# Local attention in a 12-layer stack: products P V with 64 rows of keys and the queries' values as columns, P paired by DMA, O transposed on TensorE

## The reference

```python
q, k, v = split(x @ Wqkv, 3)                  # 128 channels -> 3 * 1024
q, k = l2norm(q) * qs, l2norm(k) * ksc        # over the 64 dimensions of a head
q, k = rotary(q), rotary(k)                   # cos, sin and scale tables by token
# blocks of 32 queries; each sees its own block and the one before, 64 keys
sim = (q_block @ concat(k_prev, k_block).T) * 8.0, masked
attn = softmax(sim)                           # 32 queries x 64 keys
out = attn @ concat(v_prev, v_block)          # 64 values per head
x = x + concat_heads(out) @ Wo                # in the kernel's state
x = x + (a * gelu(gate)) @ W2 + b2            # layer norm, W1 to 2 * 341, gated
```

## Time and profile before

| what | value |
|---|---|
| time, median of 3 runs | 4463.43 us (4456.26 to 4473.81) |
| time of the profiled execution | 4466.84 us |
| its span, first to last instruction | 4465.1 us |
| busy: PE, DVE, POOL, ACT | 4085.3, 3289.0, 2496.9, 2340.3 us |
| mean granted TensorE clock | 0.972 of full speed |
| tiles in the two stacks | 192 |

### The profile page before, as it was taken

How to read it: one execution, slowest core, us unless ns; L and a number is a source line. 1 busy time by engine, 2 the same in 40 slices (tenths; PEclk the granted TensorE clock), 3 DMA queues, 4 the chain that set the end, 5 groups by cost and what they waited for, 6 DMA issues and landing times. The chain is left out here.

```text
span 4465.1 us, 195370 instructions
## 1 busy us (share of the span) xinstructions
PE 4085.3 (91%) x89528; PEld 2450.9 (55%) x89528; DVE 3289.0 (74%) x4385; ACT 2340.3 (52%) x3044; POOL 2496.9 (56%) x2036
## 2 busy tenths in 40 slices
PE   6887899999999999999678877999999999999997
PEld 2322666666666666666333335666666666666664
DVE  7997678777777877788454436777787777777774
ACT  6885455555555555555234443455555555555553
POOL 0002677776777767776200006677676776767673
PEclk8999899999999999999789998999999999999998
DMA  0001111111112112111000011112112111111110
GB/s 19 1 1 45 44 53 35 53 46 46 52 31 60 42 42 59 33 32 32 12 1 1 1 36 41 53 33 60 42 39 55 40 50 47 43 52 38 32 36 21
DMA packets 92028, 162.87 MB, mean 36 GB/s; under 512 B 33997, under 2 KB 55241, under 8 KB 91209
## 3 DMA queue, kind: packets, MB, share of 16 engines
q1 hardware_dynamic: 91208, 150.36, 12.4%
HBM read 48.61 MB, written 1.05 MB: 11 GB/s over the span
## 5 line engine op out<-in xcount | busy, mean ns | idle before, releaser
L1102 PEld LDWEIGHTS banks<-f_P_T,f_V_previous 32*64 32x64 f32 x24576 | 482.9, 131 | 509.6 <-issue 486.9
L1102 PE MATMUL banks<-f_P_T,f_V 32*64 32x32 f32 x24576 | 578.5, 223 | 35.7 <-issue 34.8
L1102 PE MATMUL banks<-f_P_T,f_V_previous 32*64 32x32 f32 x24576 | 570.0, 227 | 28.1 <-issue 24.6
L1072 PE MATMUL banks<-f_wqkv,H 128*128 128x512 f32 x1152 | 568.4, 617 | 17.0 <-DVE f_rope_bk L1395 9.5
L1341 POOL TENSOR_TENSOR f_q_rotated<-f_rope_aq,f_rope_bq 128x1024 f32<-128x1024 f32 x192 | 454.6, 2368 | 231.4 <-DVE f_rope_bq L1395 231.0
L1072 PE MATMUL banks<-f_wqkv,G 128*128 128x512 f32 x1152 | 554.0, 603 | 0.6
L1392 DVE TENSOR_TENSOR f_rope_aq<-banks,f_rope 128x1024 f32<-128x1024 f32 x192 | 235.2, 1225 | 429.6 <-ACT f_sqq L1254 415.0
L1341 POOL TENSOR_TENSOR f_k_rotated<-f_rope_ak,f_rope_bk 128x1024 f32<-128x1024 f32 x192 | 451.9, 2354 | 165.9 <-DVE f_rope_bk L1395 165.8
L1328 POOL MEMSET f_kT<- 128x256 f32 x2 | 0.6, 312 | 838.7 <-POOLq L514 460.8
L1102 PEld LDWEIGHTS banks<-f_P_T,f_V 32*64 32x64 f32 x24576 | 440.6, 133 | 41.7 <-issue 40.5
L1126 PE MATMUL banks<-f_O_T,f_wo 128*128 128x128 f32 x3072 | 437.6, 289 | 4.9 <-issue 4.9
(11 more groups left out here) (204 smaller groups left out, 8489.5 us busy)
## 6 DMA issues: line engine op xcount, KB each, us to landing
f_V_previous<-f_V SPq DMA_DIRECT2D x192, 384.0 KB, 3.6
f_V_previous<-f_V SPq DMA_DIRECT2D x192, 128.0 KB, 2.3
f_wqkv<-in_L_ffn_Wqkv SPq DMA_DIRECT2D x48, 384.0 KB, 4.1
f_rope<-in_rope SPq DMA_DIRECT2D x24, 512.0 KB, 5.2
f_wo<-in_L_ffn_Wo SPq DMA_DIRECT2D x12, 512.0 KB, 5.2
f_w<-in_L_ffn_W SPq DMA_DIRECT2D x12, 341.0 KB
f_w<-in_L_ffn_W SPq DMA_DIRECT2D x24, 64.0 KB
xin<-in_L_attn_a_x SPq DMA_DIRECT2D x2, 512.0 KB, 5.0
```

The source lines that it names most:

```text
L1072: mm = nc.tensor.matmul(ps[:, o * BLK:(o + 1) * BLK], xs, w[:, c * INNER + o * BLK:c * INNER + (o + 1) * BLK], start=True, stop=True)
L1102: mm = nc.tensor.matmul(banks[i * DH:(i + 1) * DH, g * BLK + k * W:g * BLK + (k + 1) * W], of[n % 3][r, h * DH:(h + 1) * DH], PT[n % 2][r, ...
```

## The change

`values` takes 64 keys as rows. For a pair of neighbouring query blocks (64 tokens), `F` holds the transposed P of each block with the 64 keys that it sees below one another. The stationary operand is a 64 x 32 slice of `F`, the moving one 64 rows of V or Vp with a head's 64 values as columns. There are 64 products per tile and none accumulates. The result is O with tokens on partitions, in `PQ`. ACT copies it to `O`, PE transposes it in eight 128 x 128 transposes into `PK`, and ACT evacuates that to `OT`.

`F` is made from `PT`, of which there is one in place of two, by eight transfers per tile of 32 partitions and 2 KB each (SP), and therefore values, output projection and all feed-forward steps run one slot later. `E` is laid out by side (previous block, own block) instead of by head. The products stand in two halves: one after the v projection, one after the first two feed-forward pieces; the output projection is in one piece. V has four buffers.

```diff
-            def values(n, k0, k1):
-                for k in range(k0, k1):
-                    for now, of in ((0, Vp), (1, V)):
-                        for i in range(2):
-                            h = 2 * k + i
-                            for g in range(NG):
-                                r = slice(g * W, (g + 1) * W)
+            def values(n, j0, j1):
+                for j in range(j0, j1):
+                    for a in range(2):
+                        r = slice(a * 2 * W, (a + 1) * 2 * W)
+                        for t, of in ((0, Vp), (1, V)):
+                            for hh in range(2):
+                                h = hh * (HEADS // 2) + j
+                                c = (h % 2) * HP + h // 2
+                                g = 2 * hh + t
                                 mm = nc.tensor.matmul(
-                                    banks[i * DH:(i + 1) * DH, g * BLK + k * W:g * BLK + (k + 1) * W],
-                                    of[n % 3][r, h * DH:(h + 1) * DH], PT[n % 2][r, (i * HP + k) * 2 + now, :],
-                                    start=now == 0, stop=now == 1)
+                                    PQ[g * W:(g + 1) * W, a * BLK + j * DH:a * BLK + (j + 1) * DH],
+                                    F[n % 2][r, t, c * W:(c + 1) * W], of[n % len(of)][r, h * DH:(h + 1) * DH],
+                                    start=True, stop=True)
...
 # SP, at the head of a slot
+                if live(s - 2):
+                    sp.wait_ge(ppt.sem, ppt.at(n - 2))
+                    sp.wait_ge(o_mm.sem, o_mm.past(n - 4))
+                    for a in range(0, P, 2 * W):
+                        for t in range(2):
+                            for b in range(2):
+                                sp.dma_start(F[n % 2][a + b * W:a + (b + 1) * W, t, :],
+                                             PT[a + t * W:a + (t + 1) * W, b, :]).then_inc(pair_in[n % 2].sem, 16)
...
 # PE, the slot's second part
-                if live(s - 2):
-                    values(n - 2, 2, 4)
                 feed_second(s)
-                if live(s - 2):
-                    values(n - 2, 4, 6)
+                if live(s - 3):
+                    values(n - 3, HEADS // 4, HEADS // 2)
                 feed_third(s)
-                if live(s - 3) and s % TB != 1:
-                    out_part(s, 0, HP // 2)
-                if live(s - 2):
-                    values(n - 2, 6, 8)
+                if live(s - 4):
+                    out(s)
                 feed_fourth(s)
                 if live(s - 3):
-                    out_part(s, HP // 2 if s % TB != 1 else 0, HP)
+                    if live(s):
+                        pe.wait_ge(sqd.sem, sqd.at(n))
+                        pe.wait_ge(rot.sem, rot.at(n))
+                    else:
+                        pe.wait_ge(o_ev.sem, o_ev.past(n - 4))
+                    pe.wait_ge(o_cp.sem, o_cp.at(n - 3))
+                    for k in range(HP):
+                        mm = nc.tensor.transpose(PK[:, k * P:(k + 1) * P], O[:, k * P:(k + 1) * P], ident[:])
+                    mm.then_inc(o_tr.sem, 1)
...
 # ACT, at the head of a slot, ahead of the squares of q
+                if live(s - 4):
+                    act.wait_ge(o_tr.sem, o_tr.at(n - 4))
+                    act.wait_ge(y_mm.sem, y_mm.past(n - 6))
+                    nc.scalar.activation(OT[n % 2][:].rearrange("p a k t -> p (a k t)"), PK, ACT.Copy)\
+                        .then_inc(o_ev.sem, 1)
...
 # ACT, between V and the square of the centred block, E's exponential, Ln and Exp
+                if live(s - 3):
+                    act.wait_ge(o_mm.sem, o_mm.at(n - 3))
+                    act.wait_ge(o_tr.sem, o_tr.past(n - 4))
+                    nc.scalar.activation(O[:], PQ, ACT.Copy).then_inc(o_cp.sem, 1)
...
 # ACT, after Ln and Exp: the old evacuation of O_T is gone
-                if live(s - 2):
-                    act.wait_ge(o_mm.sem, o_mm.at(n - 2))
-                    act.wait_ge(y_mm.sem, y_mm.past(n - 4))
-                    nc.scalar.activation(OT[n % 2][:].rearrange("p g k t -> p g (k t)"),
...
 # DVE
-                    dve.wait_ge(o_mm.sem, o_mm.past(n - 4))
-                    nc.vector.transpose(PT[n % 2][:].rearrange("p h t -> p (h t)"), E[n % 2][:]).then_inc(ppt.sem, 1)
+                    dve.wait_ge(pair_in[(n - 3) % 2].sem, pair_in[(n - 3) % 2].past((n - 3) // 2))
+                    nc.vector.transpose(PT[:].rearrange("p b t -> p (b t)"), E[n % 2][:]).then_inc(ppt.sem, 1)
```

More of the change, by code:

```diff
@@ L901, in ffn_stack @@
         ri = sb("row_inverse", [P, HEADS])
-        PT = [sb(f"P_T{u}", [P, 2 * HEADS, W]) for u in range(2)]
-        OT = [sb(f"O_T{u}", [P, NG, HP, W]) for u in range(2)]
+        PT = sb("P_T", [P, 2, HEADS * W])
+        F = [sb(f"P_T_paired{u}", [P, 2, HEADS * W]) for u in range(2)]
+        O = sb("O", [P, INNER])
+        OT = [sb(f"O_T{u}", [P, 2, HP // 2, P]) for u in range(2)]
         xcs = sb("x_centered", [P, BLK])
@@ L1114, in hidden, with out @@
                                  start=True, stop=True).then_inc(sem, 1)
-            def out_part(s, k0, k1):
+            def out(s):
                 n = tile(s)
[L1119 to L1126, removed]
+                if (s - 4) % LAYER == 0:
+                    pe.wait_ge(wo_in.sem, wo_in.at(call * DEPTH + layer(s - 4)))
+                if not live(s - 1):
+                    pe.wait_ge(g_add.sem, g_add.past(n - 5))
+                pe.wait_ge(o_ev.sem, o_ev.at(n - 4))
+                for k in range(HP):
+                    hh, m2 = divmod(k, HP // 2)
+                    mm = nc.tensor.matmul(bank(4, P), wo[layer(s - 4) % 2][:, k, :],
+                                          OT[n % 2][:, :, m2, hh * 2 * W:(hh + 1) * 2 * W],
                                           start=k == 0, stop=k == HP - 1)
-                if k1 == HP:
-                    mm.then_inc(y_mm.sem, 1)
+                mm.then_inc(y_mm.sem, 1)
             def feed_first(s):
-                if (b := feed(s, 7)) is not None:
+                if (b := feed(s, 8)) is not None:
                     pe.wait_ge(g_add.sem, g_add.at(first + b * TB + TB - 1))
@@ L1136, in feed_first @@
                                      start=True, stop=True).then_inc(f_xc.sem, 1)
-                if (b := feed(s, 9)) is not None:
+                if (b := feed(s, 10)) is not None:
                     if b % NBLK == 0:
@@ L1275, in _ @@
                     squares(n, 1, k_mm, PK)
-                if (b := feed(s, 10)) is not None:
+                if (b := feed(s, 11)) is not None:
                     act.wait_ge(f_gev.sem, f_gev.at(blk(b)))
@@ L1457, in _ @@
                     nc.vector.tensor_scalar(var[:], bank(5), EPS, None, ALU.add).then_inc(f_eps.sem, 1)
[L1458 removed]
+                if (b := feed(s, 9)) is not None:
                     if b % NBLK == 0:
@@ L1474, in _ @@
                                                        src[rows, cols], ALU.add, ALU.add).then_inc(h_new.sem, 1)
-                if live(s - 3):
-                    dve.wait_ge(y_mm.sem, y_mm.at(n - 3))
-                    for rows, cols in halves(s - 3, P):
-                        nc.vector.tensor_tensor(state(s - 3)[rows, cols], bank(4, P)[rows], state(s - 3)[rows, cols],
+                if live(s - 4):
+                    dve.wait_ge(y_mm.sem, y_mm.at(n - 4))
+                    for rows, cols in halves(s - 4, P):
+                        nc.vector.tensor_tensor(state(s - 4)[rows, cols], bank(4, P)[rows], state(s - 4)[rows, cols],
                                                 ALU.add).then_inc(g_add.sem, 1)
-                if (b := feed(s, 13)) is not None and b >= SLOTS // TB - NBLK:
+                if (b := feed(s, 14)) is not None and b >= SLOTS // TB - NBLK:
                     dve.wait_ge(h_new.sem, h_new.at(blk(b)))
```

124 lines of the change are left out of this document (69 added, 55 removed).

## The result

The changed kernel takes 4600.79 us (median of 4 runs, 4596.13 to 4607.32) against 4460.92 us before: a ratio of 1.0308, 95% interval 1.0295 to 1.0321. It is slower by 3.1%, where 2.5% was forecast (4573 us).

What follows compares the result with a forecast made beforehand. PE bound before; after, the ring through ACT's copy of O: 18.28 us per slot against 17.79, 94 us, plus 10 for the ends, gives 4571, 4567 against the median, 4573 with a clock allowance; range 4475 to 4735.

Steps and rivals of the forecast that it cites:

- What bounds it before: In the kernel before, PE sets the pace: 17.50 us per slot in the best four, 17.79 on average.
- the margin of 0.72 us: In the kernel before, the gap from the end of POOL's multiplication of k to PE's transposes of k, in one slot.
- The step that decides, ACT's queue: ACT's copy of O, waiting for PE's late products, delays Ln and Exp: 5.26 us from V's end to Exp's, before 4.18.
- the upper of the two bounds: For half of the new products on PE: the old products' rate, 0.79 us, where 0.70 was taken.
- the ring: Loop of k's transposes, scores, V (PE), seeds (ACT), Newton, k's multiplication (POOL): 16.93 us before, mean 18.13 after.
- the transfers hide: SP's eight pairing transfers, 0.59 us per issue, land some 13 us before the products use them; no contention in sight.
- The rival of the clock: PE's clock falls after idling, 1.5 us on the ring: 4717 us in half of the slots, 4861 in all; chance 0.20.
- stalls of PE: Stalls inside PE's runs of matmuls, 0.29 us per slot before; 0.15 was kept, with bounds 0 and 0.29.
- The ends: At each stack's end the last tile passes added issues, landing, copy and transposes: 5 us per stack, 10 us in all.
- PE stays the bound: Rival: the copy of O is off the ring, so 17.0 to 17.1 us per slot, 4331 us; chance 0.08.
- The two cancel: Rival: the ring takes 17.8 us, so the time stays the same, 4463 plus or minus 22 us; chance 0.10.
- The products overlap less: Rival: PE's new products take twice the scores' rate, 1.41 us per half, 136 us more, 4709 us; chance 0.07.

Runs made afterwards that it cites:

- e5: Kernel before plus one unused ACT copy between V and E's exponential, released by V itself: 4460.41 us, ratio 0.9994.
- e6: Kernel before plus one unused ACT copy, released by three quarters of the products but placed behind Ln and Exp of the sums: 4464.27 us (one run).
- e1: Changed kernel with ACT's copy of O moved behind Ln and Exp of the sums: 4360.95 us, ratio 0.9779 to the kernel before.
- e2: Changed kernel with all 64 products ahead of the wait for V, ACT's order untouched: 4362.3 us, ratio 0.9781 to the kernel before.
- e4: Kernel before plus one unused ACT copy between V and E's exponential, released by three quarters of the products: 4770.78 us (one run).
- e3: Changed kernel without the eight pairing transfers and their waits, F a constant: 4580.4 us, ratio 1.0269 to the kernel before.
- e7: Kernel before plus eight transfers per tile like the pairing ones, into spare tiles nobody reads: 4490.63 us, ratio 1.007.

## Why the prediction was right, and where it was off

**What bounds it before, and the margin of 0.72 us.** That PE sets the pace is right: e5 and e6 leave the kernel before at 4460 and 4464 us with more work on ACT. The margin was read in one slot, and it is 0.73 us in two kinds of slot only (medians). Where POOL takes 5.44 us it is 0.48, and in the slot with two feed-forward products 0.20, and 0.15 of each goes to the handover when it is waited for. So even with ACT's queue clear, PE's own time could not be had in those two kinds of slot, and e1 gains next to nothing in them.

**The step that decides, ACT's queue.** Right, and shown from both sides: the copy's place (e1), its release (e2), and the copy without the change (e4 to e6). Its terms: V's end to the copy 2.90 forecast (2.09 and 0.81), 2.87 measured (medians over 80 slots); seeds' end 5.26 forecast, 5.22 measured, and 5.75 against 5.70 in the slot with the square. Two errors cancel in it, which is luck: half of the products takes 0.79 us, not 0.70 (the upper of the two bounds), and the feed-forward products, now undivided, 0.96 each, not 1.02.

**The size.** The mean slot was forecast at 18.28 us and is 18.59 in the window of 80 slots. Four terms of the ring were too small or left out:

- The scores take 1.55 us on average in place of 1.45 before (1.41 in the row that was used): 0.14. That the transfers hide was right for their landing; that they leave PE alone was not, and e3 prices it at 20 us at least. Their issue was off as well: 5.92 us for eight (median of 83 slots, 5.12 to 7.79), 0.74 each, not 0.59, though still covered. One of the long ones:

```profile
1414.69 7.25 SPq L1053 DMA_DIRECT2D f_P_T_paired<-f_P_T  x8
```

- POOL's end to PE's transposes is 0.15 us, not 0.05, and the k projection behind them starts after 0.90, not 0.87: 0.13. A handover that was never waited for cannot be read off a timeline.
- In one slot of four POOL's part takes 5.46 us, not 5.13: 0.08. It did so before as well (5.44 there); the row read was of another slot. What is longer is the instruction that runs beside DVE's scaling of the centred block, here POOL's multiplication of q, 2.23 us for 1.90:

```profile
1407.13 0.76 DVE L1504 SCALAR_TENSOR_TENSOR f_xn<-f_x_centered,f_ln_g_ln_b_b,f_var_then_rstd 128x512 f32<-128x512 f32 x1
```
```profile
1407.42 2.23 POOL L1389 TENSOR_TENSOR f_q_rotated<-f_q_rotated,f_inverse_norm 128x1024 f32<-128x1024 f32 x1
```

- The clock. In 7 of the 80 slots PE's clock fell to the lower of its two levels. Six are of the kind with two feed-forward products, and their period is 19.7 to 19.9 us in place of 18.3. PE had idled 1.13 and 0.86 us before, and then most of the k transposes and of the k projection ran at the lower level (the granted clock is 0.50 from 1223 to 1225 us in the slot shown, and 1.00 again from 1226):

```profile
1220.33 1.09 PE L1228 MATMUL banks<-ident,f_q_rotated 128*128 128x128 f32 x8 [1.13 <-POOL f_q_rotated L1389]
1222.28 1.72 PE L1234 MATMUL banks<-ident,f_k_rotated 128*128 128x128 f32 x8 [0.86 <-POOL f_k_rotated L1389]
1223.79 2.96 PE L1097 MATMUL banks<-f_wqkv,H 128*128 128x512 f32 x4
```

  The seventh slot, early in the stack, had idled 2.01 and 0.77 us. 7 x 1.5 / 80 = 0.13 us per slot. The rival of the clock, priced as "1.5 us, in half of the slots or in all", had the right size per slot and came true in one of eleven.

Against these, 0.15 us that the prediction kept for stalls of PE is not seen: but for the seven slots with the fallen clock and one other, no period is over 0.5 us longer than the median of its kind. 0.14 + 0.13 + 0.08 + 0.13 - 0.15 = 0.33, and 0.31 is missing.

This sum is of the window, which overstates the miss. Over the 190 periods of both stacks the slot grew by 0.64 us, against 0.80 in the window and 0.49 forecast, since over all of them the kernel before takes more per slot than in the window (17.87 us against 17.79) and the changed one less (18.51 against 18.59). So 0.15 us per slot is what the time lacks. That the four terms keep their sizes in the second stack was not worked out.

**The ends.** Forecast 10 us, measured 14: from the last V of a stack to the first of the next 572.3 us in place of 564.5, and from the last V to the end of the span 93.3 in place of 86.9. The slots between them grew by 66.7 us in the first stack and 54.1 in the second, 121 in place of 94.

**The rivals.** *PE stays the bound*: no in this kernel. Its time of 4331 us is near what the repaired ones reach (4361, and 4301 with DVE's sum moved), but in e1 and e2 it is the ring that sets the pace. *The two cancel*: no. *The products overlap less*: no. A half, 64 records, takes 0.79 us to the start of the next instruction, 12 ns for each, where this rival had 1.41. The Trainium skill ("TensorE: Matmul & The Clock Gate", Back-to-back issue gap) gives a floor of about 25 ns per start. The trace does not agree, and the measurement decides.

## What to carry to other kernels

Before work goes to an idle engine, look at what stands behind it in that engine's order, and at when its operands come: neither a microsecond of work nor a late release costs anything alone, but a late release in front of an instruction that a ring of other engines needs lengthens every round, by all of the delay that the ring does not have in hand. When a change takes work from the engine that sets the pace, follow the next ring in full, with each handover at its price when it is waited for, since what is in hand there (0.7 us here in the best kinds of slot, 0.2 in the worst) bounds what the change can bring. Read that margin in every kind of slot. And a change that loses may be one instruction away from winning: this one went from 3.1% slower to 2.2% faster by a move of one copy, and to 3.6% faster with one sum moved too.

## What the runs showed of the hardware

The pairing transfers (64 KB each, 2 KB per partition) slow PE's scores from 1.41 to 1.61 us in the three kinds of slot in which their issue starts 0.11 us ahead of the scores. Where it starts 1.42 us (the fourth kind) or 0.97 us (e7) behind the scores' start, they take 1.41, and without the transfers they take 1.41 to 1.42 in all four (e3). The POOL instruction that runs beside DVE's 128 x 512 scaling of the centred block (0.75 us, SBUF to SBUF) is longer by 0.33 us in nearly every one of these slots: q's multiplication with 2.23 for 1.90 us in the changed kernel, Newton's last step with 0.57 for 0.25 before. Beside the feed-forward result, which DVE reads from PSUM, nothing is longer. And the clock of PE fell after idle times of 1.13 and 0.86 us, with eight transposes between them, in 6 of the window's 20 slots with two feed-forward products, and not in others with the same idle times; in e3, in 9 of 20.
